# Delta rule: queries projected once, their causal filter moved from TensorE to ACT and DVE

## What is computed

```python
def _causal_dw_conv_silu(x, w):
    y = jax.lax.conv_general_dilated(jnp.swapaxes(x, 1, 2), w[:, None, :], window_strides=(1,),
                                     padding=[(KS - 1, 0)], feature_group_count=C)
    return jax.nn.silu(jnp.swapaxes(y, 1, 2))
...
q = _causal_dw_conv_silu(x @ Wq, conv_q).reshape(bsz, seq_len, H, KD)
k = _causal_dw_conv_silu(x @ Wk, conv_k).reshape(bsz, seq_len, H, KD)
v = _causal_dw_conv_silu(x @ Wv, conv_v).reshape(bsz, seq_len, H, VD)
q = _l2norm(q)
k = _l2norm(k)
...
def step(state, inp):
    q_t, k_t, v_t, a_t, b_t = inp
    retained = jnp.einsum('bhvk,bhk->bhv', state, k_t)
    a4 = a_t[..., None, None]
    b4 = b_t[..., None, None]
    rk = retained[..., None] * k_t[:, :, None, :]
    vk = v_t[..., None] * k_t[:, :, None, :]
    state = a4 * (state - b4 * rk) + b4 * vk
    o_t = jnp.einsum('bhvk,bhk->bhv', state, q_t)
    return (state, o_t)
```

## Time and profile before

| | |
|---|---|
| Time, median of 3 runs | 4628.96 us (4626.64 to 4648.89) |
| The profiled execution's own time | 4647.18 us |
| Its span in the profile | 4645.4 us |
| Busy over the span | PE 84%, PEld 53%, DVE 51%, ACT 33%, POOL 16% |
| Mean granted clock of TensorE | 0.789 |
| Setup of the delta rule, then its 64 chunks (a chunk from one L1895 to the next) | from 2810.9; first L1895 at 2907.2, last at 4508.3 us |

### The profile page before, as it was taken

How to read it: one execution, slowest core, us unless ns; L and a number is a source line. 1 busy time by engine, 2 the same in 40 slices (tenths; PEclk the granted TensorE clock), 3 DMA queues, 4 the chain that set the end, 5 groups by cost and what they waited for, 6 DMA issues and landing times. The chain is left out here.

```text
span 4645.4 us, 124865 instructions
## 1 busy us (share of the span) xinstructions
PE 3879.7 (84%) x55640; PEld 2439.1 (53%) x55640; DVE 2377.7 (51%) x6080; ACT 1513.0 (33%) x2786; POOL 736.9 (16%) x716
## 2 busy tenths in 40 slices
PE   3647777699947887878787795999999999999986
PEld 1215665344415565656555442666666666666673
DVE  3466776333347778777776111344444444444445
ACT  2444323355532222222221242333233333333323
POOL 1121222000011212121211000222222221222210
PEclk8877667899965656565655797989899998999977
DMA  2000000322100000000000001000000000000000
GB/s 77 0 0 1 1 1 1 56 37 36 19 16 3 3 3 3 3 3 3 3 3 3 15 0 56 2 2 2 2 2 2 2 2 2 2 2 2 2 2 20
DMA packets 18967, 45.93 MB, mean 10 GB/s; under 512 B 4864, under 2 KB 8320, under 8 KB 17408
## 3 DMA queue, kind: packets, MB, share of 16 engines
q1 hardware_dynamic: 18432, 37.95, 3.6%
HBM read 35.71 MB, written 2.23 MB: 8 GB/s over the span
## 5 line engine op out<-in xcount | busy, mean ns | idle before, releaser
L1812 PE MATMUL ps<-d_hp,d_w_qk 128*128 128x512 f32 x1024 | 578.2, 662 | 2.7 <-DVE d_hp L2064 2.7
L1031 PE MATMUL ps<-g_Q,g_K 32*32 32x32 f32 (+1 forms) x12288 | 272.0, 247 | 26.9 <-issue 12.5
L1031 PEld LDWEIGHTS ps<-g_Q,g_K 32*32 32x32 f32 x12288 | 235.9, 134 | 71.6 <-PE ps L1031 38.8
L1885 POOL TENSOR_TENSOR d_sq<-d_QK 128x512 f32<-128x512 f32 x128 | 133.4, 1042 | 849.5 <-ACT d_QK L1927 791.5
L852 PE MATMUL ps<-ex_hs,w_c_fc 128*128 128x512 f32 x512 | 232.3, 597 | 19.7 <-DVE ex_hs L818 19.7
L1063 PE MATMUL ps<-g_S,g_V 32*64 32x32 f32 x4096 | 161.1, 287 | 87.4 <-DVE g_H L1239 70.0
L826 DVE TENSOR_TENSOR ex_r<-ex_r 128x512 f32<-128x512 f32 x128 | 88.4, 692 | 277.0 <-ACT ex_r L840 277.0
L863 PE MATMUL ps<-ex_r,w_c_proj 128*128 128x512 f32 x512 | 230.0, 592 | 0.0
L840 ACT ACTIVATE ex_r<-ps 128x512 f32<-128x512 f32 x256 | 151.6, 593 | 235.5 <-PE ps L852 235.5
L1905 ACT ACTIVATE d_F<-ps 128x128 f32<-128x128 f32 x256 | 70.8, 276 | 471.2 <-PE ps L1726 469.9
L1812 PEld LDWEIGHTS ps<-d_hp,d_w_qk 128*128 128x128 f32 x1024 | 172.3, 202 | 77.3 <-issue 60.1
(11 more groups left out here) (452 smaller groups left out, 8132.6 us busy)
## 6 DMA issues: line engine op xcount, KB each, us to landing
ex_root<-gate_rows SPq DMA_DIRECT2D x8, 2048.0 KB, 15.5
d_QK<-in_conv_qk_dram SPq DMA_DIRECT2D x2, 2048.0 KB, 7.1
X<-in_x_dram SPq DMA_DIRECT2D x1, 2048.0 KB, 10.9
w_c_fc<-in_c_fc_dram SPq DMA_DIRECT2D x1, 2048.0 KB, 8.2
w_c_proj<-in_c_proj_dram SPq DMA_DIRECT2D x1, 2048.0 KB, 12.6
out_dram<-X SPq DMA_DIRECT2D x1, 2048.0 KB, 6.3
w_wmod<-in_wmod_dram SPq DMA_DIRECT2D x1, 1536.0 KB, 6.5
w_w<-in_w_dram SPq DMA_DIRECT2D x2, 768.0 KB, 4.9
```

The source lines that it names most:

```text
L1031: ins = e.matmul(later(scored, n_), keys_, queries(n_, planes, r, 4 * i + j), start=(turn_ == 0 and part == 0 and n_ != 1), stop=(part == ...
L1812: ins = e.matmul(b, w_qk[:, j, c, ts(H, C)], hp_of(u)[:, j:j + T], start=(j == 0), stop=(j == TAPS - 1))
L1885: e.tensor_tensor(squares(x), qk, qk, ALU.mult).then_inc(pool.steps, pool.did(f"{tag}sq{x}"))
```

## The change

Query weights are no longer multiplied by the taps. One product of 128x512 makes the unfiltered projection of a head (at step 4), and the filter follows in four steps in the new tile `d_conv`: ACT multiplies by the last tap (piece `conv` 0, step 5, place 2), and DVE adds the bank shifted by 1, 2 and 3 columns times the other taps (pieces 1 to 3 at steps 5, 6 and 7, place 1), each on one column less. The Silu at step 8 reads `d_conv` and waits for DVE's third addition. Keys stay as they were. One of the two setup blocks goes, and a table of 128x8x4 numbers is loaded with the stage's weights.

```diff
--- before.py
+++ after.py
@@ -120,7 +120,7 @@
                  "bout_0", "W_Q", "W_K", "W_V", "W_O", "head_mask", "head_scale", "w_gate1", "rev8", "upto", "ones",
                  "c_fc", "c_proj"],
     "gla": ["W_in2", "b_in2", "W_qka", "b_qka", "W_v2", "b_v2", "W_y2", "b_y2", "W_out2", "b_out2", "h0", "gla_mask"],
-    "delta": ["Wv3", "Wg3", "Wab3", "Wo3", "A_log", "dt_bias", "conv_v", "o_norm_w", "joins", "eye32", "upto3", "ones3", "picks"],
+    "delta": ["conv_q", "Wv3", "Wg3", "Wab3", "Wo3", "A_log", "dt_bias", "conv_v", "o_norm_w", "joins", "eye32", "upto3", "ones3", "picks"],
     "mix": ["W_r3", "W_k3", "W_v3", "mu"],
     "mlp2": ["gate_w2", "w1_2", "w2_2", "b1_2", "b2_2"],
 }
@@ -1527,7 +1527,7 @@
     nc = k.nc
     TAPS, NH, NT = 4, 8, 4
     with ExitStack() as s:
-        w_qk = k.sb("d_w_qk", [C, TAPS, 2, 8 * C], stack=s)
+        w_q, w_k = k.sb("d_w_q", [C, 8 * C], stack=s), k.sb("d_w_k", [C, TAPS, 8 * C], stack=s)
         w_v = k.sb("d_w_v", [C, TAPS, 256], stack=s)
         neg_a = k.sb("d_neg_a", [C, NH], stack=s)
         hp2 = k.sb("d_hp", [C, 2, T + 3], stack=s)
@@ -1543,6 +1543,7 @@
                  ("beta", "z", "g", "t", "gc", "gam", "end", "ga", "qn", "kn", "gtot", "n2", "sp", "ms")}
         ssq = k.sb("d_ssq", [C, 2, NT, NH], stack=s)
         sq_rows = k.sb("d_square_rows", [8, T], stack=s)
+        cv = k.sb("d_conv", [C, T], stack=s)[:]
         S = k.sb("d_S", [C, NH, 32], stack=s)
         D = k.sb("d_D", [C, 2, 4, C], stack=s)
         A, Pm = (k.sb("d_" + n, [C, 6, 4, C], stack=s) for n in ("A", "P"))
@@ -1574,7 +1575,7 @@
                 e.tensor_scalar(neg_a[:], neg_a[:], -1.0, None, ALU.mult).then_inc(dve.steps, dve.did())
         k.end()
         taps = QK[:].rearrange("p c h t -> p (c h t)")[:, 0:TAPS * 8 * C].rearrange("p (j f) -> p j f", j=TAPS)
-        for n in range(2):
+        for n in (1,):
             pe, act, dve, pool, dma = k.stage(f"delta_taps{n}")
             with nc.Block() as block:
                 @block.sync
@@ -1584,9 +1585,10 @@
 
                 @block.vector
                 def _(e):
+                    e.tensor_copy(w_q[:], w_plain[:, 0]).then_inc(dve.steps, dve.did())
                     e.wait_ge(dma.steps, dma.at("taps"))
                     for j in range(TAPS):
-                        e.tensor_tensor(w_qk[:, j, n], w_plain[:, n], taps[:, j], ALU.mult).then_inc(dve.steps, dve.did())
+                        e.tensor_tensor(w_k[:, j], w_plain[:, n], taps[:, j], ALU.mult).then_inc(dve.steps, dve.did())
             k.end()
 
         f2 = lambda ap: ap.rearrange("p h t -> p (h t)")
@@ -1622,7 +1624,11 @@
                     put(u, x - 9, "norms", x)
                 for x in range(32):
                     turn = NI * (x // 8) - 50 + x % 8
-                    put(u, turn, "taps", x, place={8: 0, 1: 1}.get(turn % NI, 2))
+                    if x % 8 in (0, 4, 5, 6, 7):
+                        put(u, turn, "taps", x, place={8: 0, 1: 1}.get(turn % NI, 2))
+                for x in range(0, 8, 2):
+                    for j in range(TAPS):
+                        put(u, NI * (x // 2) - 49 + max(j - 1, 0), "conv", TAPS * x + j, place=(2 if j == 0 else 1))
                 for x in range(8):
                     put(u, NI * (x // 2) - 46 + 4 * (x % 2), "taps_done", x, place=(1 if x % 2 == 0 else 2))
                     put(u, NI * (x // 2) - 42 + 2 * (x % 2), "squares", x)
@@ -1805,11 +1811,16 @@
                         elif what == "taps":
                             run, j = x // 4, x % 4
                             c, H, b = run % 2, 4 * g + run // 2, tap_bank(run)
-                            if x == 0:
-                                e.wait_ge(dve.steps, dve.at(f"u{u - g}nh"))
+                            if c == 0:
+                                if x == 0:
+                                    e.wait_ge(dve.steps, dve.at(f"u{u - g}nh"))
+                                if u or run:
+                                    e.wait_ge(dve.steps, dve.at(f"{tag}conv{TAPS * run - 5}" if run else f"u{u - 1}conv27"))
+                                e.matmul(b, w_q[:, ts(H, C)], hp_of(u)[:, 3:3 + T], start=True, stop=True).then_inc(pe.steps, pe.did(f"{tag}run{run}"))
+                                return
                             if j == 0 and (u or run > 1):
                                 e.wait_ge(act.steps, act.at(f"{tag}run{run - 2}" if run > 1 else f"u{u - 1}run{run + 6}"))
-                            ins = e.matmul(b, w_qk[:, j, c, ts(H, C)], hp_of(u)[:, j:j + T], start=(j == 0), stop=(j == TAPS - 1))
+                            ins = e.matmul(b, w_k[:, j, ts(H, C)], hp_of(u)[:, j:j + T], start=(j == 0), stop=(j == TAPS - 1))
                             if j == TAPS - 1:
                                 ins.then_inc(pe.steps, pe.did(f"{tag}run{run}"))
                         elif what == "squares":
@@ -1922,9 +1933,16 @@
                             e.wait_ge(pe.steps, pe.at(f"{tag}values{x}"))
                             e.activation(VG[:, :, x, ts(g, 128)], ring_bank(u, "values", x)[:, 0:256].rearrange("p (v x) -> p v x", v=2),
                                          ACT.Silu).then_inc(act.steps, act.did(f"{tag}values{x}"))
+                        elif what == "conv" and x % TAPS == 0:
+                            run = x // TAPS
+                            e.wait_ge(pe.steps, pe.at(f"{tag}run{run}"))
+                            e.activation(cv, tap_bank(run), ACT.Copy, scale=k.w["conv_q"][:, 4 * g + run // 2, 3:4]).then_inc(act.steps, act.did(f"{tag}conv{x}"))
                         elif what == "taps_done":
-                            e.wait_ge(pe.steps, pe.at(f"{tag}run{x}"))
-                            e.activation(QK[:, x % 2, 4 * (u % 3) + x // 2], tap_bank(x), ACT.Silu).then_inc(act.steps, act.did(f"{tag}run{x}"))
+                            if x % 2 == 0:
+                                e.wait_ge(dve.steps, dve.at(f"{tag}conv{TAPS * x + 3}"))
+                            else:
+                                e.wait_ge(pe.steps, pe.at(f"{tag}run{x}"))
+                            e.activation(QK[:, x % 2, 4 * (u % 3) + x // 2], cv if x % 2 == 0 else tap_bank(x), ACT.Silu).then_inc(act.steps, act.did(f"{tag}run{x}"))
                         elif what == "gate" and x == 0:
                             e.wait_ge(dve.steps, dve.at(tag + "negabs"))
                             e.activation(four("beta"), four("beta"), ACT.Exp, scale=-1.0).then_inc(act.steps, act.did())
@@ -2062,6 +2080,14 @@
                             e.tensor_tensor(tmp[:, 0, :], ring_bank(u, "norm", 1), tmp[:, 1, :], ALU.mult).then_inc(dve.steps, dve.did(tag + "nx"))
                             e.wait_ge(dve.steps, dve.at(tag + "nx"))
                             e.tensor_scalar(hp_of(u)[:, 3:], tmp[:, 0, :], k.mod[:, 3, CA, b:b + 1], k.mod[:, 3, SA, b:b + 1], ALU.mult, ALU.add).then_inc(dve.steps, dve.did(tag + "nh"))
+                        elif what == "conv" and x % TAPS:
+                            run, late = x // TAPS, x % TAPS
+                            if late == 1:
+                                e.wait_ge(act.steps, act.at(f"{tag}conv{TAPS * run}"))
+                            else:
+                                e.wait_ge(dve.steps, dve.at(f"{tag}conv{x - 1}"))
+                            e.scalar_tensor_tensor(cv[:, late:], tap_bank(run)[:, 0:T - late], k.w["conv_q"][:, 4 * g + run // 2, 3 - late:4 - late], cv[:, late:],
+                                                   ALU.mult, ALU.add).then_inc(dve.steps, dve.did(f"{tag}conv{x}"))
                         elif what == "scale":
                             e.wait_ge(act.steps, act.at(f"{tag}values{x}"))
                             if x == 0:
@@ -2383,6 +2409,7 @@
 
     rows = lambda v: c(np.broadcast_to(v[None], (C,) + v.shape))
     o["Wqk3"] = c(np.stack([i["L3_attn_Wq"], i["L3_attn_Wk"]], 1))
+    o["conv_q"] = c(i["L3_attn_conv_q"].reshape(8, C, 4).transpose(1, 0, 2))
     o["conv_qk"] = c(np.stack([i["L3_attn_conv_q"].T, i["L3_attn_conv_k"].T], 0))
     o["Wv3"] = c(i["L3_attn_Wv"])
     o["conv_v"] = rows(c(i["L3_attn_conv_v"].T))
```

## The result

The changed kernel takes **4729.9 us** (median of 4 runs, 4728.2 to 4732.4). The kernel before took 4630.8 us beside it, and 4630.8 to 4638.2 us beside the runs of the experiments. The ratio is 1.0206, 95% interval 1.0187 to 1.0225: 2% slower. The forecast was 4644 us, with a range up to 4725.

The account below looks back on a forecast made before the run. TensorE was taken to bound the delta rule stage. Terms -46 + 86 - 12 - 13 = +15 us against the profiled 4647.2 us, carried over to the median 4629.0: 4644 us, range 4550 to 4725.

Parts of the forecast that it names:

- Steps 5 and 6: Setup: one of two tap-spreading blocks goes, -12 us; ahead of turn 0: 18 tap products go from TensorE, -13 us.
- Steps 1 to 3: Delta rule chunks: query products removed, filter put on ACT and DVE; net 0.8 us faster a chunk, -46 us for 58.
- step 3: A chunk's third turn, after f4: one of two tap products goes, 0.95 us gained; third multiply-add behind ze is covered.
- Step 4: TensorE's clock: a second fall in each chunk, 3.6 us more at half, priced 0.41: 1.5 us a chunk, +86 us.
- clock of 0.83: Sign of being right: TensorE's clock at 0.83 to 0.87 from 2880 to 4400 us.
- second rival: Clock stays down from behind k·k into the state stretch: 5 us more at half a chunk, +97, 4726 us; chance 0.20.

Follow-up runs that it names:

- the late version: Changed kernel with the query filter's first multiply-add moved behind ze on DVE and the two others a turn later: 4497.2 us, ratio to before 0.9687 to 0.9738.

## Why the prediction was wrong

The sum was +15 us; the profiled executions differ by +81. Of the 86 us between 4644 and 4729.9, 66 are this. The other 20 are the base: the execution shown of before lay 0.4% above its median, that of after just below its own.

- **Steps 5 and 6** (setup -12, ahead of turn 0 -13) were right in their sum, -25: the first Exp comes 29.1 us earlier. The split was not. The block of key weights begins at 2825.20 us, 20.8 us ahead of the second block of the earlier trace rows (2845.95) and 8.1 ahead of the first (2833.26), so the setup gave 20.8 us and what follows it 8.3:

```profile
2825.20 4.63 DVE L1591 TENSOR_TENSOR d_w_k<-d_QK 128x1024 f32<-128x1024 f32 x4 [7.12 <-DMA d_QK<-in_conv_qk_dram]
```

- **Steps 1 to 3** had 0.8 us a chunk, from three products gone (2.85 us) and idle time and delay of some 2 us. Measured: idle time +2.00 us a chunk, so 0.85 us. The prices held as well. Here are the two new lines in the groups of the kernel after:

```profile
L2089 DVE SCALAR_TENSOR_TENSOR d_conv<-ps,w_conv_q,d_conv x192: 736/747/751, 2841.3 to 4486.1; 128x511 f32<-128x511 f32 x64, 128x510 f32<-128x510 f32 x64, 128x509 f32<-128x509 f32 x64
...
L1939 ACT ACTIVATE d_conv<-ps,w_conv_q x64: 687/691/692, 2840.5 to 4479.4; 128x512 f32<-128x512 f32 x64
```

- One clause of **step 3** failed: "This gain stands: TensorE has the keys' transposes and one product (1.5 us) from f4 on, and ze comes 1.2 to 1.3 us after it." In the chunk shown ze ends 2.4 us after f4 has begun, and the product takes 1.92 us, so the turn gives nothing (2.64 us from f4 to the products on zz, where the earlier trace rows has 2.59). Nor would it at full clock: with one addition ahead of X the key product takes 1.02 us, ze 1.24, and the same stretch 2.44. I had read ze's 0.43 us in the earlier trace rows as its length. That steps 1 to 3 come out at 0.85 all the same is partly luck, since half clock covers most of this wait.
- **Step 4, the clock, is the term that was mis-sized.** It had 3.6 us more at half in a chunk, at 0.41: +1.5 us, +86 in all. Measured are 5.6 us more (9.2 against 3.6), at 0.44 by the late version: 2.5 us a chunk. With the 0.85 us gained that is +1.6, where the Exp rows show +1.70 (107 us in 63 chunks). The price and the sign were right, the duration was not. I expected a fall that ends before the state stretch. The clock of 0.83 that I had named as a sign of being right did come, and did not tell my sum from the second rival. In the chunk shown the clock falls behind f4 and stays down through it and beyond.
- **The cause I gave for step 4 was wrong.** I put the fall down to sparse columns, with the idle time as an addition. Without the chain the same columns run at 0.92. The Trainium skill ("TensorE: Matmul & The Clock Gate", section "HAM oscillation — how this bites in real kernels") blames waits in which the engine stands idle. I took from it that waits of 2 us would change nothing, and argued from the earlier trace rows that the trace speaks against it. Both fail. The clock falls behind waits of 1.3 to 1.9 us here, which are shorter than those that its section shows, and no longer does where they are filled (0 of 47 chunks). And the earlier trace rows begins too late. TensorE is busy for 8.00 of 8.00 us there, but just ahead it stood idle for 0.52 us, and the clock fell behind that (kernel before):

```profile
3924.00:3927.00 3.00, 2.48 (x52) 2.33 (x50) 1.11 (x5) 1.77 (x2) 1.04 (x1) 1.00 0.00 0
3927.00:3928.00 1.00, 1.00 (x11) 1.00 (x9) 0.00 (x0) 0.00 (x0) 0.00 (x0) 0.88 0.00 0
```

  What the earlier trace rows does show is that the clock can stay at half for 7 us with TensorE busy throughout. No fall without a gap ahead of it is on record.
- **The second rival** (stays down across both stretches, 4726 us, chance 0.20) is what happened, and its time is right to 4 us. Part of that is luck: its sum was +97, and between the profiled executions, for which the sums are made, it is +81. It had 5 us more at half at 0.51; there are 5.6 at 0.44. That the range ended 5 us below the result follows from giving it too little: its own condition, that one product at half speed does not lift the clock again, had no row against it.

What stays open: which gaps the clock falls behind. Ahead of f4 the same 1.28 us brings a fall in 18 chunks and none in 31, and 0.46 us brings none in 54, while 0.52 us ahead of the earlier trace rows did. Between these kernels and places the work around the gap differs too, and no run varied the gap alone. That the additions on the chain lower the clock through the gap is shown by moving them and by filling it; what else has a part in a single fall is not.
